# Moving four row sends per batch on GpSimd's queue from the fourth head group into the third

## The chip, the cores and the metric

One core of one Trainium2 chip runs the whole program. The metric is the device time of one execution in microseconds, taken without a profile; of the kernel before there are three such runs.

## What is computed

Two transformer-like layers over x of 4 batches x 512 tokens x 256 features, each with a residual:

```python
x = x + L0_attn(layernorm(x))   # latent attention, 16 heads, causal, rotary part of 64
x = x + L0_ffn(layernorm(x))    # 64 experts, top 6 of a softmax gate, plus shared experts
x = x + L1_attn(layernorm(x))   # Mamba-2 style chunked scan, 8 heads, chunks of 64
x = x + L1_ffn(layernorm(x))    # gated feed-forward, 704 wide
```

The change lies in the first line, where rows for the second are already sent. Of the attention, per head h:

```python
q = rmsnorm(x @ w_qa) @ w_qb            # nope part 128, rope part 64, rotated by cos/sin
scores = q . k * scale, masked; attn = softmax(scores); out = attn . v; out @ w_o
```

Of the experts: each token's normalised row goes to its 6 chosen experts, and the weighted results are added to x.

## The kernel before, in words

Attention runs batch by batch (b = 0 to 3), and within a batch by four head groups (hg = 0 to 3) of four heads each. A head group has 16 units: unit u is head u % 4 of the token tile u // 4 (128 tokens). Its score product is 128 queries against 128 x (tile + 1) keys, so units 0 to 3 are 128 wide and units 12 to 15 are 512 wide. The order of work is written out by hand in slots, one per unit, on every engine:

- TensorE (`slot` in `att_tensor`): scores of the unit (L521 and the mask product L522), in slots 1, 3, 5, 7 the query product of the next group (L480, L481), in slots 9, 11, 13, 15 the transposes of its query tiles (L486) after waiting for the rotation of that tile, the transposes of the probabilities three units back (L530), and at three places the products with the values (L547).
- VectorE (`slot` in `att_vector`): the negated row maximum of the unit (L853), the reciprocal of the sum before (L858), the copy of transposed probabilities (L873, L876), the scaling of the probabilities (L864). From batch 1 on it also does steps of the expert routing of the batch before, such as L1129.
- ScalarE: the exponential (L700), which signals `A["exp"]`; copies of queries (L681, L685) and values (L712).
- GpSimd (`att_pool`): the rotation of the next group's query tiles (`rope`, L964 to L968, four instructions), and the **row sends**.

A row send (`send`, L1195) is one indirect DMA that scatters 128 normalised rows of 256 values from `xn1` to the places of one expert choice in the DRAM tensor `sent`. A batch has 4 tiles x 6 choices = 24 of them. They go out while the next batch is in attention: the first waits for the routing's places and for the zeroing of `sent` (`send_ready`). Each send on GpSimd's queue is in program order with the rotations. A rotation for group hg stands on the queue at the time of group hg - 1: `turn(..., GROUPS - 1)` makes the queries of the fourth group, and runs while TensorE is in the third. After the fourth group's rotations, GpSimd waits for the exponentials of the fourth group's units, one send behind each.

Who needs the sends: VectorE overwrites `xn1` with the next batch's rows (L950, L951) only when all sends of the batch before have landed; the expert loop reads `sent` once all 96 sends are there (L1295). The last batch's 24 sends follow its attention back to back and are not touched by the change. Later, in the second layer, GpSimd gathers result rows with the same kind of indirect DMA.

Of the kernel before, what the change touches and what calls it, by code (L numbers as in the profile page):

```python
# [19 lines left out]
TB = SEQ // P  # L20
# [35 lines left out]
def build(nc, a, out):  # L56

    ctx = ExitStack()
    with ctx:
# [355 lines left out]
        NU = HG * TB  # L415
# [7 lines left out]
        def need(eng, s, value):  # L423

            if value > 0:
                eng.wait_ge(s, value)
# [528 lines left out]
        def rope(api, eng, i, parts_done, n_parts, done, tmp):  # L955

            q = qs[:, i, :].rearrange("p (h c) -> p h c", h=HG)
            ta = tmp[:, 0, :].rearrange("p (h c) -> p h c", h=HG)
            tb = tmp[:, 1, :].rearrange("p (h c) -> p h c", h=HG)
            half = DR // 2  # L960
            c = cosq[:, i, :].unsqueeze(1).to_broadcast([P, HG, DR])
            s1 = sinq[:, i, 0:half].unsqueeze(1).to_broadcast([P, HG, half])
            s2 = sinq[:, i, half:DR].unsqueeze(1).to_broadcast([P, HG, half])
            api.tensor_tensor(ta, q[:, :, KVL:QE], c, ALU.mult).then_inc(parts_done, 1)  # L964
            api.tensor_tensor(tb[:, :, 0:half], q[:, :, KVL + half:QE], s1, ALU.mult).then_inc(parts_done, 1)
            api.tensor_tensor(tb[:, :, half:DR], q[:, :, KVL:KVL + half], s2, ALU.mult).then_inc(parts_done, 1)
            eng.wait_ge(parts_done, n_parts)
            api.tensor_tensor(q[:, :, KVL:QE], ta, tb, ALU.add).then_inc(done, 1)  # L968

        def att_pool(pool):  # L970
            nc.gpsimd.memset(wqe2[QL2:P], 0.0).then_inc(consts, 1)
            nc.gpsimd.memset(cq2[QL2:P], 0.0).then_inc(consts, 1)
            n = 0

            def turn(g, i):
                nonlocal n
                pool.wait_ge(A["qs"], TB * g + i + 1)
                need(pool, A["rope_p"], n)
                rope(nc.gpsimd, pool, i, A["rope_pa"], 3 * n + 3, A["rope_p"], qtmp)
                n += 1  # L980

            for b in range(BATCH):
                for i in (0, 2):
                    turn(GROUPS * b, i)
                for hg in range(1, GROUPS):
                    for i in range(TB):
                        turn(GROUPS * b + hg, i)
                        if b and hg == GROUPS - 1:
                            if i == 0:
                                send_ready(pool, b - 1)  # L990
                            send(b - 1, 2 * i)
                            send(b - 1, 2 * i + 1)
                if b:
                    g = GROUPS * b + GROUPS - 1
                    for u in range(NU):
                        pool.wait_ge(A["exp"], NU * g + u + 1)
                        send(b - 1, 2 * TB + u)


        R = {k: sem(f"r_{k}") for k in  # L1000
# [189 lines left out]
        def send_ready(pool, c):  # L1190
            pool.wait_ge(R["slots"], c + 1)
            h = (c + 1) * SEQ > SPAN
            pool.wait_ge(zeroed[h], 16 * ZERO_PARTS + 16)

        def send(c, n):  # L1195

            t, k = TB * c + n // TOPK, n % TOPK
            nc.gpsimd.indirect_dma_start(  # L1198
                sent[:, :], bass.IndirectOffsetOnAxis(ap=slots[:, t, k:k + 1], axis=0),
                xn1[:, n // TOPK, :], None).then_inc(M["sent"], 16)  # L1200
# [953 lines left out]
        @block.gpsimd  # L2154
        def _(pool):
            for s in [M[k] for k in MCREDIT]:
                pool.sem_inc(s, START)
            for s in stored:
                pool.sem_inc(s, 16)
            nc.gpsimd.memset(zeros, 0.0).then_inc(consts, 1)  # L2160
            nc.gpsimd.memset(ones[:], 1.0).then_inc(consts, 1)
            loaded(pool, "first")
            nc.gpsimd.tensor_copy(identb[:], ident).then_inc(consts, 1)
            nc.gpsimd.tensor_copy(futureb[:], future).then_inc(consts, 1)
            pool.wait_ge(consts, 4)
            loaded(pool, "tables")
            att_pool(pool)
            send_ready(pool, BATCH - 1)
            for n in range(TB * TOPK):
                send(BATCH - 1, n)  # L2170
            loaded(pool, "ffn1")
            scale_down(pool)
            return_early(pool)
            pool.wait_ge(M["back"], 1)
            pool.wait_ge(N2.done["tr"], KC)
            ssm_pool(pool)
# [183 lines left out]
```

## Time and profile before

| | us |
|---|---|
| median of 3 runs | 1321.08 |
| lowest and highest | 1320.51, 1321.24 |
| span of the profiled execution | 1372.1 |
| TensorE busy in it | 1236.2 (90%) |
| VectorE busy | 801.9 (58%) |
| ScalarE busy | 463.7 (34%) |
| GpSimd busy | 376.6 (27%) |

The times come from executions without a profile, the busy times and every row below from one execution with it. Its span is given from the first to the last instruction of the program; what lies around the span is not known. Row times are microseconds from the span's start, with the duration behind them. The ends of TensorE's instructions are modelled, its starts are recorded. Idle time of an engine stands in square brackets, with what ended it.

### The profile page before, as it was taken

Reading aid. Unit: us, or ns where it says so; the run is one execution under the profiler, and the core shown is the slowest. Engines: PE = TensorE matmul, PEld = TensorE weight load, DVE = VectorE, ACT = ScalarE, POOL = GpSimd, SP = SyncE. Lnnn points to the kernel's source line nnn. Section 1 sums busy time; section 2 is a strip of 40 time slices with the busy share of each in tenths; the row PEclk is TensorE's granted clock in tenths of the full one; section 3 lists DMA queues with packets and bytes.
Section 4 is the critical chain, followed back from the end, with each engine's and each line's share of the span. In section 5 each row is a group of like instructions: output and inputs, shape, how many; then the busy total and the mean of one; then the engine's idle time right before and its main releaser. Section 6 shows DMA issues by size and latency. Waiting matters only on the chain.

```text
span 1372.1 us, 19483 instructions
## 1 busy us (share of the span) xinstructions
PE 1236.2 (90%) x6005; PEld 767.3 (56%) x6005; DVE 801.9 (58%) x2226; ACT 463.7 (34%) x1057; POOL 376.6 (27%) x464
## 2 busy tenths in 40 slices
PE   6999999989999899988959999997585987999988
PEld 3566566555555466556536777775244545555454
DVE  6377767786578667784513434334665673685431
ACT  2455435442455335442201111111331612625310
POOL 1242023451425413351340000113564261311200
PEclk9799999999999999999979999999777998999999
DMA  9999999999800100010336888884212021000000
GB/s 320 413 419 420 420 421 420 420 420 418 334 1 32 62 1 1 8 58 30 107 103 191 274 263 269 270 278 138 67 43 62 1 70 39 12 12 16 0 16 16
DMA packets 89422, 235.48 MB, mean 172 GB/s; under 512 B 12768, under 2 KB 23680, under 8 KB 89088
## 3 DMA queue, kind: packets, MB, share of 16 engines
q1 hardware_dynamic: 70912, 192.54, 37.9%
q0 software_dynamic: 9216, 25.18, 5.8%
q10 hardware_dynamic: 9216, 16.78, 3.2%
q8 instruction: 42, 0.69, 0.2%
q14 instruction: 36, 0.29, 0.1%
HBM read 66.70 MB, written 167.77 MB: 171 GB/s over the span
## 4 chain that ended last, share of the span: by engine, by line
PE 72%; DVE 15%; issue 4%; another core or an unknown queue 3%; ACT 2%; SPq 2%; DMA 1%; POOL 1%; ACTq 0%; DVEq 0%; POOLq 0%
PE bank L521 6%; PE bank L547 5%; PE bank L480 4%; PE bank L609 4%; PE bank L530 4%; PE bank L481 4%; PE bank L1327 4%; PE bank L1349 3%; PE bank L1588 3%; PE bank L1594 3%; DVE negmax L853 3%; PE bank L1605 3%; DVE r L864 2%; PE bank L1639 2%
## 5 line engine op out<-in xcount | busy, mean ns | idle before, releaser
L700 ACT ACTIVATE r<-bank,negmax 128x128 f32<-128x128 f32 (+3 forms) x256 | 134.9, 527 | 173.7 <-DVE negmax L853 163.5
L521 PE MATMUL bank<-r 128*128 128x512 f32 (+3 forms) x512 | 184.2, 443 | 0.0
L853 DVE TENSOR_REDUCE negmax<-bank 128x1 f32<-128x128 f32 (+3 forms) x256 | 124.1, 485 | 55.9 <-PE bank L522 53.0
L530 PE MATMUL bank<-tables,r 128*128 128x128 f32 x640 | 117.7, 284 | 19.8 <-DVE r L864 18.6
L964 POOL TENSOR_TENSOR r<-r,tables 128x256 f32<-128x256 f32 x56 | 42.0, 749 | 331.7 <-ACT r L681 331.6
L1198 POOL DMA_INDIRECT sent<-r,slots x96 | 93.9, 978 | 113.0 <-ACT r L700 49.1
L530 PEld LDWEIGHTS bank<-tables,r 128*128 128x128 f32 x640 | 75.2, 145 | 74.6 <-issue 35.6
L1436 DVE COPY r<-bank 128x512 f32<-128x512 f32 x64 | 41.2, 685 | 116.3 <-PE bank L1358 75.3
L864 DVE TENSOR_SCALAR r<-r,rrow 128x128 f32<-128x128 f32 (+3 forms) x256 | 103.8, 406 | 0.3
L521 PEld LDWEIGHTS bank<-r 128*128 128x128 f32 x512 | 77.8, 191 | 23.6 <-issue 18.4
L1214 POOL DMA_INDIRECT r<-sent,slots x16 | 15.2, 950 | 223.3 <-DMA sent<-r 219.6
L480 PE MATMUL bank<-r 128*128 128x512 f32 x128 | 70.7, 634 | 3.6 <-DVE x L808 1.5
L1550 POOL TENSOR_TENSOR r<-tables,r 128x1024 f32<-128x1024 f32 x16 | 31.2, 1960 | 153.6 <-DVE r L1969 123.6
L873 DVE COPY late<-bank 128x256 f32<-128x256 f32 (+1 forms) x128 | 60.4, 472 | 16.5 <-PE bank L530 16.5
L481 PE MATMUL bank<-r 128*128 128x512 f32 x128 | 66.6, 602 | 0.0
L1394 ACT ACTIVATE r<-bank 128x512 f32<-128x512 f32 x32 | 19.1, 597 | 137.1 <-PE bank L1327 125.0
L1327 PE MATMUL bank<-r 128*128 128x256 f32 x256 | 62.4, 388 | 0.0
L1349 PE MATMUL bank<-r 128*128 128x256 f32 x256 | 61.3, 382 | 0.0
L609 PE MATMUL bank<-spent,r 128*128 128x256 f32 x256 | 57.9, 383 | 0.5 <-ACT r L712 0.5
L522 PE MATMUL bank<-futureb,identb 128*128 128x128 bf16 x256 | 56.1, 219 | 0.0
L609 PEld LDWEIGHTS bank<-spent,r 128*128 128x128 f32 x256 | 47.8, 190 | 11.8 <-issue 4.6
L1349 PEld LDWEIGHTS bank<-r 128*128 128x128 f32 x256 | 48.0, 190 | 8.9 <-issue 2.7
(276 smaller groups left out, 2404.4 us busy)
## 6 DMA issues: line engine op xcount, KB each, us to landing
sent<-gath SPq DMA_DIRECT2D x8, 16384.0 KB, 88.1
r<-waT_dram SPq DMA_DIRECT2D x64, 304.0 KB, 3.1
r<-sent SPq DMA_DIRECT2D x64, 256.0 KB
sent<-r ACTq DMA_DIRECT2D x64, 256.0 KB
w2buf<-wcT_dram SPq DMA_DIRECT2D x64, 48.0 KB, 3.5
r<-w_o_dram SPq DMA_DIRECT2D x1, 2048.0 KB, 11.2
sent<-gath SPq DMA_DIRECT2D x2, 1024.0 KB, 56.7
out_dram<-x SPq DMA_DIRECT2D x4, 512.0 KB, 2.9
```

Of the source, the lines that this page charges most:

```text
L480: nc.tensor.matmul(bank[at][:], cq1[:, i * P:(i + 1) * P], w1, start=True, stop=False)
L481: nc.tensor.matmul(bank[at][:], cq2[:, i * P:(i + 1) * P], w2, start=False, stop=True)\
L521: nc.tensor.matmul(at[:, 0:n], QT[g % 2][:, h, i * P:(i + 1) * P], KT[:, 0:n], start=True, stop=False)
L530: last = nc.tensor.transpose(bank[TRANS[u % 2]][:, j * P:(j + 1) * P], prob[:, u % 4, j * P:(j + 1) * P], ident)
L547: last = nc.tensor.matmul(bank[VALUE][KVL * half:KVL * (half + 1), c:c + 2 * P], V[:, j, :], p[:, 2 * half:2 * half + 2, :].rearrange("p h ...
L609: last = nc.tensor.matmul(bank[4 + i % 2][:, 0:DIM], OT[:, c, i * P:(i + 1) * P], wvo[:, c, :], start=(c == 0), stop=(c == HEADS // 2 - 1))
L700: nc.scalar.activation(prob[:, u % 4, 0:(i + 1) * P], bank[SCORE[u % 4]][:, 0:(i + 1) * P], ACT.Exp, bias=negmax[:, u:u + 1], scale=1.0, a ...
L853: nc.vector.tensor_reduce(negmax[:, u:u + 1], bank[SCORE[u % 4]][:, 0:(i + 1) * P], axis=AX.X, op=ALU.max, negate=True).then_inc(A["max"], 1)
L864: nc.vector.tensor_scalar(p, p, rrow[:, u:u + 1], None, ALU.mult).then_inc(A["norm"], 1)
L1198: nc.gpsimd.indirect_dma_start(sent[:, :], bass.IndirectOffsetOnAxis(ap=slots[:, t, k:k + 1], axis=0), xn1[:, n // TOPK, :], None).then_in ...
L1327: last = nc.tensor.matmul(bank[2][:, t * ROWS:(t + 1) * ROWS], wb[:, 2 * q + t, k * EI:k * EI + EA], tokens(q, t, k), start=(k == 0), stop ...
L1349: nc.tensor.matmul(to[t][:, half * DIM:(half + 1) * DIM], hid_a[:, q % 2, c:c + P], wb[:, 2 * q + t, KC * EI:KC * EI + DIM], start=(half = ...
```

## The change

In batches 1 to 3, the four rotations for the fourth head group are each followed by three sends instead of two. The remaining sends, 12 instead of 16, stand behind the exponentials of units 1, 3, 5, 7 and 8 to 15 of the fourth group instead of behind all 16. The order of the sends and their number stay.

```diff
                         if b and hg == GROUPS - 1:
                             if i == 0:
                                 send_ready(pool, b - 1)
-                            send(b - 1, 2 * i)
-                            send(b - 1, 2 * i + 1)
+                            for m in range(3):
+                                send(b - 1, 3 * i + m)
                 if b:
                     g = GROUPS * b + GROUPS - 1
-                    for u in range(NU):
+                    for m, u in enumerate((1, 3, 5, 7, *range(8, NU))):
                         pool.wait_ge(A["exp"], NU * g + u + 1)
-                        send(b - 1, 2 * TB + u)
+                        send(b - 1, 3 * TB + m)
```

## Rows read from the trace of the kernel before

**Rows 1.** The page: its first line, and the chain that ended last, by engine

```profile
span 1372.1 us, 19483 instructions
...
PE 72%; DVE 15%; issue 4%; another core or an unknown queue 3%; ACT 2%; SPq 2%; DMA 1%; POOL 1%; ACTq 0%; DVEq 0%; POOLq 0%
```

**Rows 2.** Windows, fourth head group of batches 0, 1: length, busy per engine, PEclk, DMA

```profile
139.40:161.40 22.00, 21.46 (x138) 13.06 (x139) 19.62 (x68) 12.33 (x39) 0.00 (x0) 1.00 1.02 420
287.70:316.90 29.20, 23.37 (x140) 13.55 (x140) 23.50 (x100) 12.28 (x39) 14.59 (x15) 0.97 1.02 419
```

**Rows 3.** Timeline of VectorE, batch 1: start, duration, instruction, [idle before <-releaser]

```profile
298.46 0.42 DVE L853 TENSOR_REDUCE negmax<-bank 128x1 f32<-128x256 f32 x1 [3.46 <-PE bank L522]
...
308.40 0.56 DVE L873 COPY late<-bank 128x384 f32<-128x384 f32 x1 [0.71 <-PE bank L530]
...
311.52 0.69 DVE L853 TENSOR_REDUCE negmax<-bank 128x1 f32<-128x512 f32 x1 [1.42 <-PE bank L522]
```

**Rows 4.** Timeline of TensorE, batch 1: the mask product of unit 5

```profile
296.30 0.22 PE L522 MATMUL bank<-futureb,identb 128*128 128x128 bf16 x1
```

**Rows 5.** Timeline of VectorE, batch 2: the maxima of units 5 and 13

```profile
454.00 0.42 DVE L853 TENSOR_REDUCE negmax<-bank 128x1 f32<-128x256 f32 x1 [3.50 <-PE bank L522]
...
467.06 0.69 DVE L853 TENSOR_REDUCE negmax<-bank 128x1 f32<-128x512 f32 x1 [2.13 <-PE bank L522]
```

**Rows 6.** Timeline of GpSimd, batch 1, fourth group: four of its 16 sends

```profile
291.23 1.06 POOL L1198 DMA_INDIRECT sent<-r,slots  x1 [8.23 <-ACT r L700]
...
299.75 0.96 POOL L1198 DMA_INDIRECT sent<-r,slots  x1 [2.41 <-ACT r L700]
...
308.71 0.96 POOL L1198 DMA_INDIRECT sent<-r,slots  x1 [0.30 <-issue]
...
317.31 0.96 POOL L1198 DMA_INDIRECT sent<-r,slots  x1 [1.53 <-ACT r L700]
```

**Rows 7.** The chain in order of time: start, length, what it is put down to

```profile
688.61 16.82 another core or an unknown queue
...
1043.56 7.02 another core or an unknown queue
...
1127.44 12.29 another core or an unknown queue
```

**Rows 8.** Timeline of all engines, behind the last batch's sends: ScalarE resumes

```profile
705.46 0.59 ACT L1497 ACTIVATE r<-bank 96x512 f32<-96x512 f32 x1 [16.27 <-remote]
```

**Rows 9.** One source line, the sends: duration ns min/median/max, first and last start

```profile
L1198 POOL DMA_INDIRECT sent<-r,slots x96: 956/960/1186, 265.7 to 700.6; - x96
```

**Rows 10.** Timeline of GpSimd, batch 1, third group: parts of rotations 2 and 4

```profile
269.82 0.72 POOL L968 TENSOR_TENSOR r<-r 128x256 f32<-128x256 f32 x1
...
277.86 0.75 POOL L964 TENSOR_TENSOR r<-r,tables 128x256 f32<-128x256 f32 x1
...
279.62 0.80 POOL L968 TENSOR_TENSOR r<-r 128x256 f32<-128x256 f32 x1
```

**Rows 11.** Timeline of TensorE, batch 1, third group: transposes of rotated tiles 2, 4

```profile
278.02 0.63 PE L486 MATMUL bank<-tables,r 128*128 128x128 f32 x4 [0.52 <-issue]
...
286.60 0.63 PE L486 MATMUL bank<-tables,r 128*128 128x128 f32 x4 [0.84 <-ACT r L685]
```

**Rows 12.** Timeline of VectorE, end of batch 1: the next rows for the experts

```profile
346.36 1.38 DVE L339 TENSOR_SCALAR r<-x,mv,rstd 128x256 f32<-128x256 f32 x4 [0.35 <-ACT rstd L334]
```

**Rows 13.** Timeline of VectorE, batch 1, third group: scalings and routing steps

```profile
277.00 0.41 DVE L864 TENSOR_SCALAR r<-r,rrow 128x384 f32<-128x384 f32 x1
...
278.19 1.05 DVE L864 TENSOR_SCALAR r<-r,rrow 128x384 f32<-128x384 f32 x1
...
279.56 0.27 DVE L1129 SCALAR_TENSOR_TENSOR scratch<-r,scratch 128x64 f32<-128x64 f32 x1
...
279.77 0.73 DVE L1129 SCALAR_TENSOR_TENSOR scratch<-r,scratch 128x64 f32<-128x64 f32 x1
```

**Rows 14.** Windows, end of batch 2's fourth group, columns as in rows 2

```profile
468.80:475.60 6.80, 6.38 (x28) 4.14 (x29) 5.59 (x20) 1.93 (x5) 2.88 (x3) 0.50 0.17 60
```

## The prediction

> **What bounds the kernel now.** I read the page first: its span, and the chain that ended last. The chain is nearly three quarters TensorE and a seventh VectorE; GpSimd holds 1% of it [rows 1]. Twelve relocated GpSimd instructions can count only through what they delay on those two engines. So next I took the busy times of stretches in which row sends run. The fourth head group of batch 0 has no sends: from its first score product to its last exponential it takes 22.0 us. Batch 1 with 16 sends takes 29.2 us, batches 2 and 3 the same within 0.1 [rows 2]. Of the 7.2 us more, VectorE's busy time explains 3.9 (23.50 against 19.62, routing steps added to those slots); the other 3.3 are VectorE's idle time, 5.70 against 2.38.
>
> The timelines show where. In batch 1 VectorE's maximum of unit 5 starts at 298.46 after 3.46 us idle [rows 3]. It waits for the mask product of TensorE that the trace has at 296.30 with 0.22 us, so done by 296.52 [rows 4]: the release came 1.94 us late. Later the copy at 308.40 waits 0.71 and the maximum of unit 13 at 311.52 waits 1.42 us, again for TensorE work that was over [rows 3]. Batch 2 repeats it at the same two units, idle 3.50 and 2.13 us [rows 5], and batch 3 within 0.1 us of that. Both places come after unbroken runs of sends: five between the idle times ahead of the sends at 291.23 and 299.75, then eight from 299.75 to 308.71, which is 8.96 us over 7 steps, some 1.28 us for one [rows 6]. I call these late releases **holds**: TensorE has finished, GpSimd issues, and the release is not seen. They are 3 x 1.94 = 5.8 us at unit 5 (batch 1's value taken for all three), and 0.71 + 1.42 + 2 x 2.13 = 6.4 us at unit 13.
>
> The chain in order of time has three larger pieces of this kind, put down to "another core or an unknown queue": 16.82, 7.02 and 12.29 us, 36.1 in all [rows 7]. Each stands in or just behind a run of GpSimd's indirect DMAs. In the first, ScalarE is idle for 16.27 us until 705.46 [rows 8]; the last of the 24 sends that run there back to back starts at 700.6 [rows 9].
>
> **The number that decides.** All holds together are 5.8 + 6.4 + 36.1 = 48.3 us. The profiled execution's span is 1372.1 us [rows 1]; the median of the runs without a profile is 1321.08 us, 51.0 less. The profiled execution is longer by almost exactly what it holds, and I found nothing else of this size in it. My reading is that the holds belong to the profiled execution and are largely absent from the timed ones. No row proves this; it is a coincidence of two sums, and gets no more than three chances in five for that reason.
>
> The Trainium skill, "NOTIFIC — the notification-queue block", section 7.1, says that the block which writes an execution's records does not lose one inside its own pipeline but pushes back, and that this can throttle an engine. That is a way in which recording could make holds; no row here shows the record queue. The page supports the forecast and gives no term of it.
>
> **The change, part by part.** Batches 1 to 3 keep 24 sends each (those of the batch before); four per batch move from units 0, 2, 4 and 6 of the fourth group into the third. No instruction is added or removed. The 24 sends behind the last batch stay, and with them the 16.82 us of the profile.
>
> (1) *Third group: three sends behind each rotation, not two.* At 1.28 us for a send, rotations 2, 3 and 4 come 1.3, 2.6 and 3.8 us later. In batch 1 rotation 2 ends at 269.82 + 0.72 = 270.54, so 271.8 after; TensorE transposes its tile at 278.02. Rotation 4 ends at 279.62 + 0.80 = 280.42, so 284.3 after; TensorE comes to it at 286.60, where it waits for ScalarE [rows 10, 11]. The slack left is 6.2 and 2.3 us, and that of rotation 3 lies between. Cost 0. If that cover is gone, each microsecond is paid on TensorE's in-order queue, in three batches. The three sends behind rotation 4 then end near 284.3 + 3.8 = 288.1, before unit 0's exponential let a send go at 291.23 [rows 6].
>
> (2) *Fourth group: waits on units 0, 2, 4 and 6 gone, on the other twelve kept.* Behind them on GpSimd's queue stand only sends and then the next batch's rotations. The last send follows unit 15 as before, at 317.31 [rows 6]. VectorE overwrites the sent rows from 346.36 on, 29 us later [rows 12]. Cost 0.
>
> (3) *The port between VectorE and GpSimd.* A rotation does slow VectorE. The 128x384 scaling at 278.19, beside the rotation begun at 277.86, took 1.05 us against 0.41 at 277.00; a routing step behind it 0.73 against 0.27 just before [rows 10, 13]. That is 0.64 + 0.46 = 1.1 us. Sends show nothing alike on their side: 956 ns at least, 960 at the median [rows 9]. Rotations that move meet other instructions of VectorE, so the term lies between -1.1 and +1.1 us a batch, -3.3 to +3.3 us in all. I take 0: rotation 4 leaves one set of routing steps and lands near the next.
>
> The Trainium skill, "SBUF — State Buffer", section on the three doors with its "DVE blocks DMA" trap, says that GpSimd, writing descriptors, and VectorE's two-port instructions lock each other out of one port pair. It speaks against sends beside a busier VectorE; by that rule the four moved sends a batch would cost up to the bound of (3) and the sum would be 1324.4 us. The rotations' rows agree with it, the sends' durations don't.
>
> (4) *The holds.* Sends behind every second unit leave no run of five ahead of unit 5. From unit 7 on one per unit remains, a run of up to eight. In the third group runs become three, broken by rotations of 2.4 us. In the profile I expect the unit 5 holds to go (-5.8 us, a span near 1366) and the unit 13 holds to stay or shrink. In the timed runs: 0, by the comparison of sums.
>
> The sum for the timed runs is 1321.1 + 0 + 0 + 0 + 0 = **1321.1 us**. Its own range is 1318.4 to 1323.7, which is also the 0.2% that a measurement of this kernel can tell from no change.
>
> **Rivals.** *The holds are real in timed runs too.* Then those of unit 5 go: 1321.1 - 5.8 = 1315.3. If the lighter load ends those of unit 13 as well, 1308.9. Behind these the clock was granted at 0.50, the lower level, for 6.8 us in batch 2 [rows 14], as long in batch 3 and half as long in batch 1, 17 us in all; that is worth at most half, 8.5 us: 1300.4. For it: the rows repeat in three batches. Against it: the 51.0 us. *The holds are real, and runs of three make new ones in the third group.* If it brings two of 1.94 us a batch for the one removed, + 5.8 us: 1326.9. It decides if three sends are enough; the shortest run ahead of a hold is five. *Rotation 4 comes late.* Its slack of 2.3 us is read in a profiled execution. It decides if TensorE reaches slot 15 more than 2.3 us sooner after rotation 1 without a profile; at 3.5 us sooner it would wait 1.2 us in each batch: +3.6, 1324.7. Against it: the third group has no hold whose absence would speed it up. *Port collisions add up*: +3.3, 1324.4.
>
> **How the numbers follow.** The forecast, within 0.2%, gets 0.58. Real holds get 0.27, all faster: 0.18 near 1315, 0.09 between 1300 and 1311. Slower gets 0.15: late rotation or port 0.10, new holds 0.05. The range takes in 1315.3 with part of a port term below it, to 1313.5, and 1325.0 above; 0.09 and 0.05 stay out, and a little at the edges.
>
> **What would show it.** In the profile of the changed kernel: no idle time above 1 us ahead of unit 5's maximum in the fourth groups (4); rotation 4 ends near 284.3 in batch 1 and TensorE doesn't wait for it (1); the span falls to about 1366 while the timed median stays. If the median falls about as much as the span, the comparison of sums misled me. If the third group lengthens, it is a wait for a rotation, or a hold there.

## The result and the profile after

The changed kernel takes 1322.62 us at the median of 19 runs, the kernel before 1319.41 us in 19 runs beside them. The ratio is 1.0025, 95% interval 1.0017 to 1.0033. That is 3.2 us slower by the medians and 3.3 by the ratio: inside the stated range, on the slower side of the point. By the ratio it is just beyond the 0.2% that was called no change, and 0.2% still lies in the interval. The kernel before had 1321.08 us in the three runs that the prediction knew and 1319.41 in these 19.

The page after, its first line and the chain that ended last, by engine (answering rows 1):

```profile
span 1322.4 us, 19483 instructions
...
PE 67%; DVE 19%; issue 5%; POOL 2%; SPq 2%; ACT 2%; DMA 1%; POOLq 0%; ACTq 0%; DVEq 0%
```

The span is 1322.4 us where rows 1 have 1372.1, though the timed runs went up. "Another core or an unknown queue" is gone, and with it everything of rows 7 and 8. The two profiles can't be compared as they stand. A second profiled execution of the kernel before (first experiment) has a span of 1317.5 us and none of these pieces either; it is the one to compare with, and is called **before, second profile** from here on.

Windows, second profile of before: third head groups of batches 1, 2 and 3 from first score product to the next group's, then the fourth group of batch 2, then all of attention from the first mask product to the last exponential. Columns as in rows 2.

```profile
257.60:288.14 30.54, 28.80 (x162) 17.44 (x163) 25.21 (x92) 15.28 (x46) 17.68 (x24) 1.00 1.03 420
409.29:439.45 30.16, 28.77 (x162) 17.44 (x163) 24.29 (x91) 15.34 (x46) 17.55 (x24) 1.00 0.10 36
560.60:590.77 30.17, 28.77 (x162) 17.43 (x163) 24.31 (x91) 15.35 (x46) 17.57 (x24) 1.00 0.10 36
439.45:464.47 25.02, 22.67 (x142) 13.13 (x139) 23.31 (x98) 12.21 (x40) 14.59 (x15) 1.00 0.22 79
...
59.57:615.77 556.20, 533.18 (x2843) 324.38 (x2842) 416.42 (x1379) 263.84 (x733) 196.84 (x287) 1.00 0.60 246
```

The same windows of the changed kernel:

```profile
257.37:288.59 31.22, 28.77 (x162) 17.40 (x163) 25.99 (x90) 15.29 (x46) 21.59 (x28) 1.00 1.03 420
410.08:441.18 31.10, 28.93 (x163) 17.42 (x163) 25.66 (x91) 15.36 (x46) 21.31 (x28) 1.00 0.15 52
562.59:593.68 31.09, 28.93 (x163) 17.43 (x163) 25.64 (x91) 15.36 (x46) 21.31 (x28) 1.00 0.15 52
441.18:466.46 25.28, 22.70 (x141) 13.10 (x139) 23.60 (x98) 12.24 (x40) 10.59 (x11) 1.00 0.16 58
...
59.38:618.96 559.58, 533.64 (x2843) 324.05 (x2842) 420.85 (x1379) 264.13 (x733) 196.17 (x287) 1.00 0.60 245
```

Attention is 559.58 - 556.20 = 3.4 us longer, which is the whole of the measured 3.2. Of it the third groups have 0.68 + 0.94 + 0.92 = 2.5 us, the fourth groups the rest, 0.26 in batch 2. TensorE's busy time hardly moves; VectorE's grows by 4.4 us in attention, with the same 1379 instructions. So VectorE's instructions became longer, mainly in the third groups (+0.78, +1.37, +1.33).

These are single executions, but the stages repeat. Measured from VectorE's first maximum of the third group to its first of the fourth, batches 1, 2 and 3, the second profile of before has 29.61, 29.49 and 29.49 us and the changed kernel 30.39, 30.40 and 30.40. Two more profiles of the changed kernel, on other chips than that one of before, give the same within 0.04 us, and so does a kernel that is as before from batch 1 on (the one with the port test, below), profiled on the same chip as one of them: 29.62, 29.48 and 29.49.

The timelines name the longer instructions. GpSimd and VectorE of the changed kernel, batch 2, third group; each pair is a rotation's first step and the scaling beside it:

```profile
427.81 0.74 POOL L964 TENSOR_TENSOR r<-r,tables 128x256 f32<-128x256 f32 x1
427.85 1.27 DVE L864 TENSOR_SCALAR r<-r,rrow 128x256 f32<-128x256 f32 x1
428.50 0.47 POOL L965 TENSOR_TENSOR r<-r,tables 128x128 f32<-128x128 f32 x1
...
434.02 0.75 POOL L964 TENSOR_TENSOR r<-r,tables 128x256 f32<-128x256 f32 x1
434.07 1.33 DVE L864 TENSOR_SCALAR r<-r,rrow 128x384 f32<-128x384 f32 x1
```

Rotation 3 begins 0.04 us ahead of a scaling, which ends at 429.12 instead of after 0.34 us, behind the rotation's second step too (428.50 + 0.47 = 428.97). Rotation 4 does the same to a later one, 1.33 us against 0.41. In the second profile of before, rotation 3 of batch 2 lengthens nothing, and beside rotation 4 stand smaller pieces. The worst of these, the first of which had started 0.38 us ahead of the rotation, beside the last send:

```profile
428.85 0.69 DVE L864 TENSOR_SCALAR r<-r,rrow 128x384 f32<-128x384 f32 x1
429.23 0.89 POOL L964 TENSOR_TENSOR r<-r,tables 128x256 f32<-128x256 f32 x1
...
431.29 0.73 DVE L1129 SCALAR_TENSOR_TENSOR scratch<-r,scratch 128x64 f32<-128x64 f32 x1
```

The chain of the changed kernel goes through the long scalings: of its stretch from 425 to 441 us, its view gives

```profile
427.93 1.19 DVE r L864
...
434.15 1.25 DVE r L864
```

In the fourth group smaller collisions appear with the sends themselves (all engines, changed kernel, batch 2):

```profile
452.78 0.96 POOL L1198 DMA_INDIRECT sent<-r,slots  x1 [0.75 <-ACT r L700]
453.33 0.50 DVE L864 TENSOR_SCALAR r<-r,rrow 128x256 f32<-128x256 f32 x1
```

A scaling that starts 0.55 us into a send takes 0.50 instead of 0.35 us (the one at 452.21, between sends, took 0.35). The next two take 0.56 and 0.49 for 0.41. That is 0.38 us of lengthening. The second profile of before has such pairs too, with 0.16 us in all, so 0.22 are new, and the group is 0.26 longer.

The moment of the start decides. In the nine traces of this case that show no holds, 135 scalings of attention start within 0.5 us of a send's start, and none takes over 0.02 us more than usual; 91 start 0.55 to 0.7 us into a send and take 0.02 to 0.16 more, the less the later. The four rotation steps have such a phase too: 147 scalings that start 0.50 to 0.55 us into the first or last of them (0.7 to 0.9 us long) lose 0.02 us at most, and those that start within 0.05 us of the first one's start lose 0.5 to 0.9.

### The profile page after: what moved, and what is told of

Same layout as the page of the kernel before. It is cut to its first block, busy times and chain, and to the rows that moved or that the text cites. A ratio compares the mean times of both kernels' runs of the same rounds, so it can differ in the third digit from the quotient of the medians.

```text
span 1322.4 us, 19483 instructions
## 1 busy us (share of the span) xinstructions
PE 1224.0 (93%) x6005; PEld 759.5 (57%) x6005; DVE 809.2 (61%) x2226; ACT 463.3 (35%) x1057; POOL 378.3 (29%) x464
## 4 chain that ended last, share of the span: by engine, by line
PE 67%; DVE 19%; issue 5%; POOL 2%; SPq 2%; ACT 2%; DMA 1%; POOLq 0%; ACTq 0%; DVEq 0%
PE bank L521 5%; PE bank L609 4%; PE bank L480 4%; PE bank L481 4%; PE bank L547 4%; PE bank L1349 4%; PE bank L1327 4%; DVE r L864 3%; DVE negmax L853 3%; PE bank L1588 3%; PE bank L1594 3%; PE bank L530 3%; PE bank L1605 3%; PE bank L1639 2%; PE bank L1358 2%
## 5 line engine op out<-in xcount | busy, mean ns | idle before, releaser
L1436 DVE COPY r<-bank 128x512 f32<-128x512 f32 x64 | 41.2, 686 | 116.2 <-PE bank L1358 71.8
L864 DVE TENSOR_SCALAR r<-r,rrow 128x128 f32<-128x128 f32 (+3 forms) x256 | 109.4, 427 | 0.3
L521 PEld LDWEIGHTS bank<-r 128*128 128x128 f32 x512 | 77.8, 191 | 23.6 <-issue 18.3
L1428 DVE COPY r<-bank 128x512 f32<-128x512 f32 x64 | 41.3, 683 | 23.3 <-PE bank L1312 22.1
```

Of the source, the lines that this page charges most:

```text
L521: nc.tensor.matmul(at[:, 0:n], QT[g % 2][:, h, i * P:(i + 1) * P], KT[:, 0:n], start=True, stop=False)
L864: nc.vector.tensor_scalar(p, p, rrow[:, u:u + 1], None, ALU.mult).then_inc(A["norm"], 1)
```

## The experiments

The chips used fall into two kinds: on three the kernel before takes about 1319 us, on one 1369 us. Ratios are always against the kernel before on the same chip. Each chip was used in one stretch of time only, so "kind of chip" is a name here; that it is the chip, and not something passing, was not tested.

**The kernel before, profiled again.** No edit.

> The kernel before, unchanged, for a second profiled execution of it. Theory (the holds belonged to one profiled execution, as the profile of the changed kernel without any suggests): ratio 1.000, and a span near 1319 instead of 1372.1, without the pieces of 16.8, 7.0 and 12.3 us and without idle times above 1 us ahead of the maxima of units 5 and 13. Rival (the holds belong to runs of five and more sends): the span is near 1372 again with the same pieces.

Measured: 1319.49 us, ratio 0.9998 (0.9985 to 1.0012), span 1317.5. VectorE, batch 2, the only idle time of the fourth group's timeline that answers to rows 5:

```profile
448.08 0.42 DVE L853 TENSOR_REDUCE negmax<-bank 128x1 f32<-128x256 f32 x1 [1.57 <-PE bank L522]
```

Unit 5's maximum waits 1.57 us, not 3.50, and unit 13's not at all. (The mark of 1 us, here and in the prediction, was set too low: 1.55 us stand ahead of unit 5 in the changed kernel too, an ordinary wait.) The difference at unit 5, 1.93 us, is the hold as it was worked out. The large pieces of rows 7 are missing. So the theory holds in its main point: holds are not a property of this kernel's queue order alone. That they belong to *one profiled execution*, as it was put, fell with the fifth experiment.

**The two halves of the change.** Threes in the third group, the twelve others behind units 0 to 11:

```diff
-                    for m, u in enumerate((1, 3, 5, 7, *range(8, NU))):
+                    for u in range(NU - TB):
                         pool.wait_ge(A["exp"], NU * g + u + 1)
-                        send(b - 1, 3 * TB + m)
+                        send(b - 1, 3 * TB + u)
```

> First half of the change alone: three sends behind each rotation, the other 12 behind units 0 to 11 with none left out. Theory (the time goes where rotations 3 and 4, shifted by the extra sends, meet VectorE instructions of the third group): as slow as the change, ratio 1.0025 (+3.3 us), third group 0.8 to 0.9 us longer than before in each of batches 1 to 3. Rival (it is the sends' new places in the fourth group): 1.000.

Pairs in the third group, the sixteen others at the change's places:

```diff
-                    for u in range(NU):
+                    for m, u in enumerate((1, 1, 3, 3, 5, 5, 7, 7, *range(8, NU))):
                         pool.wait_ge(A["exp"], NU * g + u + 1)
-                        send(b - 1, 2 * TB + u)
+                        send(b - 1, 2 * TB + m)
```

> Second half alone: two sends behind each rotation as before, the 16 others at the change's places in the fourth group, two each behind units 1, 3, 5 and 7. Theory (shifted rotations): ratio 1.000, third group as before. Rival (places in the fourth group): 1.0025.

Measured: threes alone 1.0011 (1.0000 to 1.0022), places alone 0.9995 (0.9985 to 1.0004). The timed runs barely part them; the attention windows do:

```profile
57.92:616.30 558.38, 533.51 (x2843) 324.36 (x2842) 419.59 (x1379) 263.81 (x733) 197.71 (x288) 1.00 0.61 247
```

for threes alone, +2.2 us against 556.20, and

```profile
59.40:615.87 556.47, 533.37 (x2842) 324.69 (x2842) 416.78 (x1379) 263.83 (x732) 196.54 (x287) 1.00 0.60 246
```

for places alone, +0.3 us. Most of the cost is in the threes. From first maximum to first maximum their third groups have 30.39, 30.40 and 30.42 us, the change's lengths, as expected; their fourth groups (22.72 us to the last exponential in batch 2) are those of before (22.76), where the change has 23.03 and places alone 22.87. So the two halves don't add up to 3.4: the fourth group's part needs both. The expected 1.0025 for threes alone was too high.

**Rotations first.** All four rotations, then the twelve sends of the third group, then as in the change:

```diff
-                        if b and hg == GROUPS - 1:
-                            if i == 0:
-                                send_ready(pool, b - 1)
-                            for m in range(3):
-                                send(b - 1, 3 * i + m)
...
+                    send_ready(pool, b - 1)
+                    for m in range(3 * TB):
+                        send(b - 1, m)
```

> All four rotations of the third group without sends between them, then the 12 sends, the rest as in the change. Theory (port collisions of the rotations): rotation 4 moves from 281.9 to about 274.0 in batch 1 and no longer meets the routing steps of 283 to 284, but meets those of 275.2 to 276.1, so 0.999 to 1.001 of before and about 2 to 3 us below the change. Rival (three more sends in the third group cost by themselves): as slow as the change, 1.0025.

Measured: 1315.96 us, ratio 0.9976 (0.9964 to 0.9989), faster than both kernels. The windows, third group of batch 2 and all of attention:

```profile
408.22:437.71 29.49, 28.59 (x163) 17.43 (x163) 23.63 (x93) 15.37 (x46) 17.45 (x24) 1.00 0.09 32
...
59.53:613.48 553.95, 532.26 (x2843) 324.12 (x2842) 414.28 (x1379) 264.17 (x733) 196.82 (x287) 1.00 0.61 247
```

The same twelve sends stand in the third group as in the change, and it is 1.6 us shorter (31.10 against 29.49). Its scalings now have a largest value of 481 ns, against 691 before and 1328 in the change. So it is not the sends in the third group that cost, but the rotations that they push onto VectorE's scalings. It came out below what was expected.

**Which rotation.** The counts behind the four rotations are varied, the twelve others stay at the change's places. First 3, 1, 5, 3:

```diff
-                            for m in range(3):
-                                send(b - 1, 3 * i + m)
+                            for m in range((3, 1, 5, 3)[i]):
+                                send(b - 1, (0, 3, 4, 9)[i] + m)
```

> The change with 3, 1, 5 and 3 sends behind the four rotations: rotation 2 at the change's time, rotation 3 back at the time of the kernel before, rotation 4 at the change's time. Theory (the port: in batch 2 rotation 3 of the change starts 0.04 us ahead of a VectorE scaling, which takes 1.27 us and not 0.34): the third group of batches 2 and 3 falls from 31.1 to 30.2 us as before, ratio about 1.0005. Rival (rotation 4, 3.8 us later, is what costs): stays 31.1 us, 1.0025.

Then 2, 4, 3, 3, by the same edit:

> The counterpart, 2, 4, 3 and 3 sends: rotation 2 at the time of the kernel before, rotations 3 and 4 at the change's. Theory: the scaling of 1.27 us stays, the third group stays at 31.0 to 31.2 us, ratio 1.0025. Rival (rotation 2's shift costs): falls to about 30.2 us, 1.0005.

These ran on the other kind of chip, where the kernel before takes 1369.29 us. Ratios: 0.9884 (0.9849 to 0.9918) and 0.9900 (0.9861 to 0.9938). The medians are 1354.77 and 1357.06 us, of six runs each that overlap; their attention takes 557.93 and 559.49 us, so the version with rotation 3 at its old time is 1.6 us faster there. Their third groups of batch 2, in that order, with edges read to 0.2 us (from mask product to mask product they are 30.54 and 31.09 us):

```profile
408.40:438.90 30.50, 28.74 (x162) 17.21 (x160) 25.42 (x88) 15.44 (x46) 21.18 (x28) 1.00 0.13 48
```

```profile
409.80:440.90 31.10, 28.94 (x163) 17.24 (x161) 25.23 (x90) 15.54 (x46) 21.30 (x28) 1.00 0.14 49
```

So rotation 3's place is worth some 0.55 us of the 0.94, and 0.5 to 0.6 in the other batches. The remaining 0.4 over the expected 30.2 is the rival's share: scalings beside rotation 4 (from 432.38) and the send ahead of it take 0.85 and 0.58 us for 0.41, a routing step 0.75 for 0.27. With rotation 3 back, VectorE comes to rotation 4 earlier, so the two places can't be priced apart. Rotation 2's place is worth nothing, as expected.

The larger finding is the 1.2% and 1.0%. Neither trace has a hold in its attention part: unit 5's maximum waits 1.55 us, an ordinary wait. Both still have pieces like those of rows 7 in the later parts (6.36, 2.86, 6.75 and 10.72 us in the first). The profile of rows 1 to 14, with its span of 1372.1 us, fits this kind of chip and no other here, though its chip is not on record. Attention has 569.40 us in it, against 557.93 and 559.49: 11.5 and 9.9 us less, holds and the half clock behind them. That is most of the 14.5 and 12.2 us of the medians; the rest lies behind attention, where nothing was changed and the pieces differ from trace to trace. So on this chip holds are part of the timed runs, and those of attention go with these patterns of sends.

The number of sends in a row alone doesn't make a hold: the version with 3, 1, 5 and 3 issues five in a row in batch 2, from 426.30 to 431.41, and VectorE isn't idle beside them.

**Four sends behind each rotation**, the other eight behind units 8 to 15:

```diff
-                            for m in range(3):
-                                send(b - 1, 3 * i + m)
+                            for m in range(4):
+                                send(b - 1, 4 * i + m)
...
-                    for m, u in enumerate((1, 3, 5, 7, *range(8, NU))):
+                    for m, u in enumerate(range(8, NU)):
                         pool.wait_ge(A["exp"], NU * g + u + 1)
-                        send(b - 1, 3 * TB + m)
+                        send(b - 1, 4 * TB + m)
```

> Four sends behind each rotation, the other 8 behind units 8 to 15 of the fourth group. Rotation 4 comes 7.6 us later than before, so ends near 288.0 in batch 1, while TensorE came to its tile at 286.60. Theory (order on GpSimd's queue): TensorE now waits for rotation 4, 1 to 1.5 us in each batch, seen as idle time ahead of its fourth tile transposes, third group 31.5 to 32.5 us, ratio about 1.003 to 1.005. Rival (TensorE is not held by rotations at all): third group as in the change or shorter.

On the second kind of chip, ratio 0.9967 (0.9938 to 0.9997), less than the two above gain. The ratio doesn't test the theory, since this chip's late releases are in it: in each batch a copy early in the fourth group waits 1.05 to 1.08 us behind four sends in a row (batch 1: until 293.41, for a product over by 292.50). The timelines do. GpSimd's rotation 4 and TensorE's transposes of its tile, batch 1:

```profile
286.76 0.79 POOL L968 TENSOR_TENSOR r<-r 128x256 f32<-128x256 f32 x1
```

```profile
287.60 0.66 PE L486 MATMUL bank<-tables,r 128*128 128x128 f32 x4 [2.67 <-POOL r L968]
```

The rotation ends at 287.55; TensorE had been ready since 284.93 and waits 2.67 us, twice what was expected; the third groups of batches 1 and 2 are 32.8 and 32.3 us long. In the change this wait doesn't occur: TensorE, batch 1, answering rows 11:

```profile
287.25 0.63 PE L486 MATMUL bank<-tables,r 128*128 128x128 f32 x4 [0.61 <-ACT r L685]
```

**Rotations first, then 24 sends with hardly a pause**: the version above with the twelve last sends behind units 0 to 11.

> Rotations first, then 12 sends, then one send behind each of units 0 to 11 of the fourth group. Theory (both effects are separate: the third group's follows the rotations, the fourth's the sends' phase): third group 29.5 us as with rotations first, the fourth group 24.97 to 25.07 us, ratio 0.997 to 0.998, the best so far. Rival (the gain needs the pauses in the fourth group): 1.000.

Again on the second kind of chip: 1.0132 (1.0089 to 1.0176), 18 to 20 us slower than before and 2.5% above the version with 3, 1, 5, 3. Neither theory foresaw that. The chain of this kernel shows holds inside attention, all in the third head groups (batches 1 and 2):

```profile
282.94 3.63 another core or an unknown queue
291.23 1.74 another core or an unknown queue
444.81 2.01 another core or an unknown queue
```

Twelve sends run from 275.84 to 290.13, one per 1.3 us, and the first hold begins during the sixth. From first maximum to first maximum the third groups take 35.25, 37.10 and 37.14 us, 6.9 to 8.6 us more than the same rotations and twelve sends take on the other kind of chip (28.33, 28.56 and 28.56, rotations first); the fourth groups are 1.6 to 2.5 us longer than with threes alone. On this kind of chip the long run costs, as the prediction's fourth part had it; on the other twelve in a row didn't. This version itself was not measured there.

**The change again**, beside the port test and once more beside the last version:

> The change itself once more. On a chip of the first kind (kernel before near 1319 us) both theories say 1.0025. On a chip of the second kind (kernel before near 1369 us, with late releases behind runs of sends): theory (the change takes the runs of five and eight out of the fourth group, and with them the holds there and the half clock behind them) 0.988 to 0.992, no hold in the attention part of its trace. Rival (those holds stay, one per unit from unit 8 on is a run too): 0.996 to 1.003.

> The change once more, beside the version above on the same chip. On a chip of the first kind 1.002 to 1.003. On one of the second kind (kernel before near 1369 us): theory (no runs of five ahead of unit 5, pauses ahead of unit 13) 0.988 to 0.992 without holds in the attention part. Rival (the run from unit 8 on still holds): 0.996 to 1.003.

Both landed on chips of the first kind: 1.0020 (1.0009 to 1.0032) and 1.0030 (1.0019 to 1.0040). With the first result that is three measurements that agree on about 0.25%. The change itself on a chip of the second kind was not measured. The version with 2, 4, 3 and 3 sends, which differs from it by the place of one send per batch, has attention as long there (559.49 us) as the change has on the first kind (559.58), without a hold.

**The port by itself.** In the kernel before, where batch 0 has no sends in its fourth group:

```diff
+        dosed = sem("dosed")
...
+                if not b:
+                    pool.wait_ge(A["rope_p"], n)
+                    for u in range(NU):
+                        pool.wait_ge(A["exp"], NU * (GROUPS - 1) + u + 1)
+                        nc.gpsimd.tensor_tensor(qtmp[:, 0, :], tables[:, 0:2 * P], tables[:, 0:2 * P],
+                                                ALU.mult).then_inc(dosed, 1)
+                        pool.wait_ge(dosed, u + 1)
```

> The kernel before, with one extra GpSimd instruction behind each exponential of the fourth head group of batch 0, where there are no sends: a 128x256 product of two SBUF operands, of the size of a rotation's first step, its result unused. It measures the port by itself. Theory (a GpSimd instruction that starts ahead of a VectorE scaling holds it back until it ends): the scalings of that group take 0.3 to 0.7 us longer wherever they start inside one, and the group (21.75 us from first score to last exponential) is 2 to 8 us longer. Rival (it is not the port, the slow scalings before come from something else): the scalings keep 0.28, 0.34, 0.41 and 0.48 us, and the group 21.75 us.

It was executed once, with its profile (1320.59 us). One pair, all engines:

```profile
143.05 0.61 POOL L999 TENSOR_TENSOR r<-tables 128x256 f32<-128x256 f32 x1 [0.72 <-ACT r L700]
143.17 0.57 DVE L864 TENSOR_SCALAR r<-r,rrow 128x128 f32<-128x128 f32 x1
```

A scaling that starts 0.12 us behind a GpSimd instruction takes 0.57 us instead of 0.27. Two others were caught, at 145.96 (0.36) and 149.23 (0.48 for 0.34). It goes the other way too: where the scaling starts first (141.38), the GpSimd instruction behind it (141.50) takes 0.82 us instead of 0.61. The other scalings keep their times, one that starts 0.59 us into a GpSimd instruction among them. The window of the group is 22.2 against 21.8 us in the second profile of before. So it is shown that instructions of the two engines lengthen each other; the size, 0.4 us, is far below the 2 to 8 that were expected, because only a start early inside the other counts. That a shared port is the reason stays an argument: the traces show who waits, not for what.

**A version for both kinds of chip.** Rotations early, and no long runs:

```diff
-                            for m in range(3):
-                                send(b - 1, 3 * i + m)
+                            for m in range((0, 1, 0, 4)[i]):
+                                send(b - 1, (0, 0, 1, 1)[i] + m)
...
+                    for m, u in enumerate(range(9, NU)):
+                        pool.wait_ge(A["exp"], NU * (g - 1) + u + 1)
+                        send(b - 1, 5 + m)
```

> A version meant to beat both: rotations at their early times (only one send between rotations 2 and 3), four sends behind rotation 4, one behind each of units 9 to 15 of the third group, and the change's 12 in the fourth. Theory (port collisions of late rotations cost in the third group, runs of sends cost only on a chip with late releases): third group 29.5 to 29.8 us, ratio 0.9970 to 0.9985 on a chip of the first kind; on one of the second kind no hold in the attention part and 0.984 to 0.990. Rival (sends among the third group's units collide with scalings themselves): 0.9990 to 1.0010 on a chip of the first kind.

On the first kind: 1316.96 us, ratio 0.9985 (0.9976 to 0.9995), with attention as short as with rotations first:

```profile
61.49:615.33 553.84, 532.20 (x2843) 324.07 (x2842) 414.38 (x1379) 263.86 (x733) 197.08 (x287) 1.00 0.60 246
```

It beats both kernels there, the changed one by 0.44% on the same chip (1316.96 against 1322.72). The ratio is at the slow end of what was expected, and no better than rotations first. What it does on the second kind was not measured.

## Why the prediction was right, and where it was not

*What bounds it.* Right: moved GpSimd instructions count only through what they delay on TensorE and VectorE. It was VectorE.

*The number that decides.* The step's outcome was right, its reason wrong. The timed runs did contain no holds. But not because a profile adds 51 us: by all that the runs show, profile and times had come from the two kinds of chip. On the second kind the timed median is 1369.29 us, and an execution with a span of 1353.1 us took 1354.99, so the span and what lies around it differ by about 1.9 us. Had I known the profiled execution's own time, the coincidence of 48.3 and 51.0 us would have read as what it is, the holds' share of the gap between two chips (1372.1 against 1317.5 us). That the forecast held is luck to this extent: on the other kind of chip its nearest relatives were 12 and 14.5 us faster, outside the range. The sign named for it, a span near 1366, didn't come; the span was 1322.4.

*Part 1, rotations late.* Right. Rotation 4 of the change ends at 283.65 + 0.73 = 284.38 (284.3 predicted); TensorE was ready for it at 286.64 and waits for ScalarE until 287.25. The fours showed the wait that begins when that slack is used up.

*Part 2, the fourth group.* A miss of about 0.3 us a batch. It looked for waits on GpSimd's queue and found none, rightly; in batch 2 the VectorE instructions are 0.29 us longer, 0.22 of it scalings that meet sends.

*Part 3, the port.* This is the term that was mis-sized: 0 taken, inside bounds of -3.3 to +3.3. The third groups measured +2.5 and the fourth groups +0.8, together the rival "port collisions add up" almost to the tenth. That is partly chance: its 1.1 us a batch was for one rotation's collisions, and the sends' 0.8 us were not in it. The change itself cost 3.2 us; the measured 1322.62 lies only 1.5 above the point because the median of the kernel before fell by 1.7 with more runs. The choice of 0 rested on "rotation 4 leaves one set of routing steps and lands near the next", and didn't lay the shifted rotations over VectorE's timeline. It was possible: rotation 3, 2.5 us later, covers 275.5 to 278, and VectorE's timeline had a two-operand product there. VectorE, batch 1, the profile of rows 1 to 14, then the changed kernel:

```profile
275.68 0.42 DVE L1123 TENSOR_TENSOR r<-r,scratch 128x256 f32<-128x256 f32 x1
```

```profile
275.87 1.16 DVE L1123 TENSOR_TENSOR r<-r,scratch 128x256 f32<-128x256 f32 x1
```

The prediction's last sign, that a longer third group would be a wait for a rotation or a hold, left this out and failed: it is neither. The statement that sends show nothing alike looked only at the sends' own duration, which is the side that doesn't wait.

The Trainium skill, "SBUF — State Buffer", in the section with the "DVE blocks DMA" trap, has a rule on that port pair that spoke against the change: of a two-port VectorE instruction and a GpSimd instruction, the one that starts first has the pair for its whole length, and the other is blocked. The runs agree that the later one waits, 1.27 us instead of 0.34 across two steps of a rotation. They differ in two points. The prediction took the rule for the moved sends, and most of the cost is the rotations'. And a scaling that starts 0.50 us or more into a step of 0.7 to 0.9 us is not lengthened.

*Part 4, the holds.* For chips of the second kind it was right in direction: the patterns closest to the change have none in attention. The unit 13 holds went too, which was expected as "stay or shrink". The rival "the holds are real in timed runs too" is what happens there: in attention 11.5 us less for 3, 1, 5, 3, near its 12.2 without the clock's part, and 14.5 us in the timed medians. The two profiles of before differ in attention by 569.40 - 556.20 = 13.2 us, which is what the holds and the half clock behind them cost there.

*Open.* What distinguishes the two kinds of chip, and what makes releases late beside sends on one of them, no run here tells; nor why five sends in a row had none in one place and twelve had several in another. What the change itself does there was not measured.

## What to carry to other kernels

When an instruction moves in time on GpSimd's queue, lay its new interval over VectorE's timeline: what stands behind it on the queue moves too, and a rotation that started 0.04 us ahead of a VectorE scaling here cost it 0.9 us. Put the work that others wait for first on such a queue, and the work that nobody waits for behind it. A long unbroken run of indirect DMAs cost nothing on one kind of chip and over 1% on the other.

A profile and a time are evidence for each other only if they come from one chip; check the span against the time of the same execution first.

## What had not been expected of the hardware

- Two kinds of chip: one program takes 1319 us on three of them and 1369 us on a fourth, and the traces of the fourth show pieces of up to 14.5 us put down to an unknown queue, beside runs of GpSimd's indirect DMAs. The edit with 3, 1, 5 and 3 sends is 1.2% faster there, and twelve sends in a row ahead of twelve more are 1.3% slower.
- A scaling that starts 0.04 us behind a rotation ends behind two of its steps: 1.27 us instead of 0.34. One that starts 0.55 us into a row send loses 0.15 us, one that starts in its first 0.5 us loses nothing.
